# The gated experts' layer written as one flat sequence of items

## The reference

```python
x = x + _L2_ffn_ref(_layernorm(x, axis=-1), ...)

def _L2_ffn_ref(hidden, router_w, router_b, sw1, sb1, sw2, sb2, rw1, rb1, rw2, rb2):
    ...
    router_logits = flat @ router_w + router_b
    router_probs = jax.nn.softmax(router_logits, axis=-1)
    topk_probs, topk_idx = jax.lax.top_k(router_probs, TOP_K)
    weights = jnp.zeros_like(router_probs).at[jnp.arange(T)[:, None], topk_idx].add(topk_probs)
    sh = jax.nn.gelu(flat @ sw1 + sb1, approximate=False)
    shared_out = (sh @ sw2 + sb2) / N_SHARED
    h1 = jax.nn.gelu(jnp.einsum('td,edh->teh', flat, rw1) + rb1[None], approximate=False)
    expert_out = jnp.einsum('teh,ehd->ted', h1, rw2) + rb2[None]
    mixed = jnp.einsum('ted,te->td', expert_out, weights)
    return (shared_out + mixed).reshape(b, s, d)
```

## Time and profile before

| | |
|---|---|
| median of 3 runs | 1946.27 us (1944.13 to 1948.13) |
| profiled execution, its own time | 1944.69 us |
| its span, first to last instruction | 1942.6 us |
| mean granted PE clock | 0.901 of full speed |
| busy over the span | PE 1607.9 us (83%), DVE 1188.3 (61%), ACT 814.8 (42%), POOL 568.0 (29%) |
| the experts' layer in the span | from 1088.4 to about 1268 us |

### The profile page before, as it was taken

One profiled execution on the slowest core, in us unless ns is written; L12 is line 12 of the kernel. 1 busy time (PEld: TensorE's weight loads), 2 busy tenths in 40 slices (PEclk: granted clock), 3 DMA queues, 4 the chain that ended last, 5 costly groups with the idle time before them and its releaser, 6 DMA issues. The chain is left out here.

```text
span 1942.6 us, 35018 instructions
## 1 busy us (share of the span) xinstructions
PE 1607.9 (83%) x12418; PEld 1087.6 (56%) x12476; DVE 1188.3 (61%) x4278; ACT 814.8 (42%) x1765; POOL 568.0 (29%) x737
## 2 busy tenths in 40 slices
PE   6796678888789998478888799978867778999888
PEld 4474434555368777454444477745545645677556
DVE  5586454772769996445655233347848875998532
ACT  2342362664248686532545433315643400333422
POOL 2132214310144444216330000032112125777121
PEclk8887878999689998789999889979988978999999
DMA  2000004210257677306220000032110000000000
GB/s 79 12 1 10 30 1 126 57 30 1 72 192 266 230 264 242 136 14 167 60 59 11 18 1 0 1 88 58 47 64 1 1 1 1 3 3 3 1 1 22
DMA packets 81334, 115.16 MB, mean 59 GB/s; under 512 B 8464, under 2 KB 62736, under 8 KB 80400
## 3 DMA queue, kind: packets, MB, share of 16 engines
q0 software_dynamic: 18432, 67.38, 9.8%
q1 hardware_dynamic: 60144, 44.45, 8.3%
q10 hardware_dynamic: 2592, 1.18, 0.3%
HBM read 88.40 MB, written 1.05 MB: 46 GB/s over the span
## 5 line engine op out<-in xcount | busy, mean ns | idle before, releaser
L2758 POOL DMA_INDIRECT f_rows<-tree_table,f_index x128 | 129.0, 1008 | 185.5 <-PE f_ps_y L2959 89.0
L3031 ACT ACTIVATE f_rows<-f_rows,f_low_act 128x128 f32<-128x128 f32 x512 | 152.9, 386 | 0.8
L1782 ACT ACTIVATE x_probs<-x_ps_z 128x768 f32<-128x768 f32 (+1 forms) x128 | 117.3, 917 | 85.6 <-PE x_ps_z L1642 57.6
L2959 PE MATMUL f_ps_y<-f_rows,shared_sb 128*128 128x128 f32 x1024 | 128.3, 288 | 29.2 <-ACT f_rows L3031 29.2
L2959 PEld LDWEIGHTS f_ps_y<-f_rows,shared_sb 128*128 128x128 f32 x1024 | 123.7, 202 | 34.9 <-ACT f_rows L3031 31.6
L82 POOL TENSOR_TENSOR rstd<-moments,shared_sb 128x14 f32<-128x14 f32 (+3 forms) x22 | 4.6, 207 | 471.3 <-DVE moments L66 471.3
L2858 DVE CUSTOM_DVE_ANT_0 f_rows<-f_rows,f_xn 128x128 f32<-128x128 f32 x512 | 111.2, 286 | 22.8 <-DMA f_rows<-tree_table,f_index 22.8
L1472 DVE TENSOR_REDUCE x_minus_max<-x_ps_s 128x4 f32<-128x1024 f32 x64 | 77.8, 1223 | 73.0 <-PE x_ps_s L1642 72.8
L2210 PE MATMUL f_ps_h<-f_xnT,weights 128*128 128x512 f32 x144 | 77.6, 667 | 2.2 <-ACT f_hT L2275 2.2
L2275 ACT ACTIVATE f_hT<-f_ps_h,weights 128x512 f32<-128x512 f32 x72 | 48.6, 685 | 70.4 <-PE f_ps_h L2210 68.6
L2222 PEld LDWEIGHTS f_ps_y<-weights,f_hT 128*128 128x128 f32 x576 | 69.7, 192 | 14.3 <-issue 12.6
(11 more groups left out here) (666 smaller groups left out, 4106.6 us busy)
## 6 DMA issues: line engine op xcount, KB each, us to landing
x_queries<-x_pieces SPq DMA_DIRECT2D x96, 64.0 KB, 2.1
x_keys<-x_pieces SPq DMA_DIRECT2D x84, 64.0 KB, 2.1
a_queries<-a_pieces SPq DMA_DIRECT2D x48, 64.0 KB, 2.1
weights<-w_L_ffn SPq DMA_DIRECT2D x1, 2953.5 KB, 9.6
a_keys<-a_pieces SPq DMA_DIRECT2D x42, 64.0 KB, 2.1
weights<-w_L_ffn SPq DMA_DIRECT2D x1, 2449.0 KB, 9.8
weights<-w_L_ffn SPq DMA_DIRECT2D x1, 2176.0 KB, 9.0
f_rows<-tree_table,f_index POOLq DMA_INDIRECT x128, 6.0
```

The costliest lines, as they stand in the source:

```text
L1782: a.activation(probs[:, r % HELD, :, :], ps_z[:, :, 0:WIDE], ACT.Exp, scale=scale).then_inc(exped, 1)
L2758: pool.indirect_dma_start(rows[:, place(u, j), tree, :], None, g.tree_table, bass.IndirectOffsetOnAxis(index[:, u % 2, low, j * TREES + tr ...
L2959: last = pe.matmul(ps_y[:, u % SUMS, j, :], g.ident, rows[:, place(u, j), tree, OUT + f * D:OUT + (f + 1) * D], start=False, stop=(low, j, ...
L3031: last = a.activation(row, row, ACT.Copy, scale=low_act[:, u % 3, j * TREES + tree, f:f + 1])
```

## The change

The layer is written as 36 items in one sequence, with no loop: the up products of item i are followed by the down products of item i-1 across the turns' borders too. The sum banks `ps_y` become three, the `hT` buffers six, and `xnT`, `chosen`, `probs` and `chosenT` hold all tiles. The tokens of turns 2 to 4 are turned behind the ups of items 1, 2 and 3 (counted from 0). Routing is done in two batches: tiles 0 to 3 ahead of the first item, tiles 4 to 15 behind the ups of item 4, with DVE's part ahead of its addition of item 3. The router's bias becomes an addition on DVE. The chosen weights get a ninth column of ones and are turned by transposes behind items 6, 12, 13 and 14; one product per tile with a matrix of nine bias rows then opens each shared item's bank. DVE measures each turn behind its last addition and aggregates it one item into the next turn.

The diff, with removed lines shown only where they say something that the listing above does not show at a glance:

```diff
--- before.py
+++ after.py
...
-    CHUNKS = ITEMS * CH
+    ALL = TURNS * ITEMS
+    HELD, SUMS = 6, 3
+    FIRST_TILES, REST_TILES = slice(0, TILES), slice(TILES, NT)
+    TOKENS_AT = {1: 1, 2: 2, 3: 3}
+    ROUTER_AT = 4
+    CHOSEN_AT = {6: 0, 12: 1, 13: 2, 14: 3}
...
+        top, chosen = sb("top", [P, NT, 8]), sb("chosen", [P, NT, ITEMS])
+        probs, rest = sb("probs", [P, NT, E + 6]), sb("rest", [P, NT, E + 6])
+        chosenT = sb("chosenT", [ITEMS, TURNS, COLS])
+        hT = sb("hT", [P, HELD, COLS])
+        ps_t, ps_r = ps("ps_t", [P, COLS]), ps("ps_r", [P, NT, E])
+        ps_h, ps_y = ps("ps_h", [P, 2, COLS]), ps("ps_y", [P, SUMS, TILES, D])
...
+        turned = [("tokens", 0)] + [("tokens", t) for t in TOKENS_AT.values()] + [("chosen", t) for t in CHOSEN_AT.values()]
+        taken = lambda kind, t: turned.index((kind, t)) + 1
+        batch_of = lambda t: min(t, 1)
...
+            step = Chain(v, steps)
+            v.memset(chosen[:, :, E:ITEMS], 1.0)
             v.memset(probs[:, :, E:E + 6], -1.0).then_inc(padded, 1)
-            v.wait_ge(padded, 1)
...
-                v.wait_ge(routed, t + 1)
-                step(v.tensor_reduce(peak[:, :], ps_r[:, :, :], AX.X, ALU.max))
-                v.tensor_tensor(probs[:, :, 0:E], ps_r[:, :, :], per_token(peak), ALU.subtract).then_inc(shifted, 1)
...
-                for e in range(ITEMS):
-                    v.wait_ge(down_made, t * ITEMS + e + 1)
-                    if e > 0:
-                        v.wait_ge(added, t * ITEMS + e)
-                    if e < E:
...
+            def normalise_turn(t):
+                if t >= 2:
+                    v.wait_ge(xT_made, t - 1)
+                normalise(v, g, t, xn[:, t % 2, :, :]).then_inc(xn_ready, 1)
+
+            def route(batch, tiles):
+                n = tiles.stop - tiles.start
+                per_token = lambda a: a[:, tiles].rearrange("p (n o) -> p n o", o=1).broadcast_to([P, n, E])
...
+                bias = w["router_b"].rearrange("p (o e) -> p o e", o=1).broadcast_to([P, n, E])
+                v.wait_ge(routed, batch + 1)
+                step(v.tensor_tensor(odds, ps_r[:, tiles, :], bias, ALU.add))
+                step(v.tensor_reduce(peak[:, tiles], odds, AX.X, ALU.max))
+                v.tensor_tensor(odds, odds, per_token(peak), ALU.subtract).then_inc(shifted, 1)
+                v.wait_ge(exped, batch + 1)
+                step(v.tensor_reduce(total[:, tiles], odds, AX.X, ALU.add))
+                step(v.reciprocal(total[:, tiles], total[:, tiles]))
+                step(v.tensor_tensor(odds, odds, per_token(total), ALU.mult))
...
+                for j in range(tiles.start, tiles.stop):
+                    last = v.max(top[:, j, :], probs[:, j, 0:E])
+                step(last)
+                step(v.memset(top[:, tiles, 2:8], -1.0))
+                v.memset(scratch[:, :], 0.0)
+                for j in range(tiles.start, tiles.stop):
+                    last = v.match_replace(rest[:, j, :], top[:, j, :], probs[:, j, :], -2.0)
...
+                step(v.tensor_tensor(chosen[:, tiles, 0:E], rest[:, tiles, 0:E], odds, ALU.not_equal))
+                v.tensor_tensor(chosen[:, tiles, 0:E], chosen[:, tiles, 0:E], odds, ALU.mult).then_inc(chosen_ready, 1)
+
+            def add(i):
+                t, e = divmod(i, ITEMS)
+                v.wait_ge(down_made, i + 1)
+                if e == 0:
+                    v.wait_ge(chosen_ready, batch_of(t) + 1)
+                else:
+                    v.wait_ge(added, i)
+                if e < E:
+                    for j in range(TILES):
...
+                        last = v.scalar_tensor_tensor(g.x[:, n, :], ps_y[:, i % SUMS, j, :], chosen[:, n, e:e + 1],
...
+                    last = v.tensor_tensor(tiles_of(g.x, t), tiles_of(g.x, t), ps_y[:, i % SUMS, :, :], ALU.add)
+                last.then_inc(added, 1)
...
+            def measure(t):
                 v.wait_ge(added, (t + 1) * ITEMS)
-                step(take_stats(v, g, t))
-                step.end()
...
-            with v.Fori(0, TURNS - 1) as t:
-                turn(t, False)
-            turn(TURNS - 1, True)
+                take_stats(v, g, t).then_inc(stats_taken, 1)
+
+            normalise_turn(0)
+            v.wait_ge(g.loaded["L2_ffn"], 16)
+            normalise_turn(1)
+            route(0, FIRST_TILES)
+            normalise_turn(2)
+            normalise_turn(3)
+            for i in range(ALL):
+                if i == ROUTER_AT - 1:
+                    route(1, REST_TILES)
+                add(i)
+                t, e = divmod(i, ITEMS)
+                if e == E:
+                    measure(t)
+                if e == 1 and t >= 1:
+                    v.wait_ge(stats_taken, t)
+                    aggregate_behind(v, g, t, TILES)
+            v.wait_ge(stats_taken, TURNS)
+            aggregate(v, g, range((TURNS - 1) * TILES, NT)).then_inc(g.aggregated, 1)
...
-            def up(t, i):
-
-                pe.wait_ge(gelu_ready, t * CHUNKS + max(i - 1, 0))
-                pe.matmul(ps_h[:, i % 2, :], w["up"][:, i * P:(i + 1) * P], xnT[:, :], start=True, stop=True).then_inc(up_made, 1)
...
-                pe.wait_ge(gelu_ready, t * CHUNKS + CH * (e + 1))
-                pe.wait_ge(added, t * ITEMS + max(e - 1, 0))
-                if e == E:
-                    pe.wait_ge(chosenT_ready, t + 1)
...
-                    if e == E:
-                        pe.matmul(out, g.ones[0:1, 0:P], w["shared_b2"], start=False, stop=False)
-                        last = pe.matmul(out, chosenT[:, j * P:(j + 1) * P], w["expert_b2"], start=False, stop=True)
...
-                pe.wait_ge(chosenT_ready, t)
+                if t >= 1:
+                    pe.wait_ge(turned_taken, taken("tokens", t) - 1)
...
+            def turn_chosen(t):
+                pe.wait_ge(chosen_ready, batch_of(t) + 1)
+                pe.wait_ge(turned_taken, taken("chosen", t) - 1)
                 for j in range(TILES):
-                    pe.matmul(ps_r[:, j, :], xnT[:, j * P:(j + 1) * P], w["router"], start=True, stop=False)
-                    last = pe.matmul(ps_r[:, j, :], g.ones[0:1, 0:P], w["router_b"], start=False, stop=True)
+                    last = pe.transpose(ps_t[0:ITEMS, j * P:(j + 1) * P], chosen[:, t * TILES + j, :], g.ident)
+                last.then_inc(chosenT_made, 1)
+
+            def score_experts(tiles):
+                for n in range(tiles.start, tiles.stop):
+                    t, j = divmod(n, TILES)
+                    if j == 0:
+                        pe.wait_ge(turned_taken, taken("tokens", t))
+                    last = pe.matmul(ps_r[:, n, :], xnT[:, t, j * P:(j + 1) * P], w["router"], start=True, stop=True)
                 last.then_inc(routed, 1)
...
-                    if e == 5:
-                        pe.wait_ge(chosen_ready, t + 1)
-                        for j in range(TILES):
-                            last = pe.matmul(ps_t[0:E, j * P:(j + 1) * P], chosen[:, j, :], g.ident, start=True, stop=True)
-                        last.then_inc(chosenT_made, 1)
-                    if e == E and not is_last:
-                        turn_tokens(t + 1)
-                    if e > 0:
-                        down(t, e - 1)
...
+            def up(i):
+                t, e = divmod(i, ITEMS)
+                for c in range(CH):
+                    k = i * CH + c
+                    if k >= 2:
+                        pe.wait_ge(gelu_ready, k - 1)
+                    pe.matmul(ps_h[:, k % 2, :], w["up"][:, (e * CH + c) * P:(e * CH + c + 1) * P], xnT[:, t, :],
+                              start=True, stop=True).then_inc(up_made, 1)
+
+            def down(i):
+                t, e = divmod(i, ITEMS)
+                pe.wait_ge(gelu_ready, CH * (i + 1))
+                if i >= SUMS:
+                    pe.wait_ge(added, i - SUMS + 1)
+                if e == E:
+                    pe.wait_ge(turned_taken, taken("chosen", t))
+                    for j in range(TILES):
+                        pe.matmul(ps_y[:, i % SUMS, j, :], chosenT[:, t, j * P:(j + 1) * P], w["b2"], start=j == 0, stop=False)
+                for j in range(TILES):
+                    for c in range(CH):
+                        at = (e * CH + c) * P
+                        last = pe.matmul(ps_y[:, i % SUMS, j, :], hT[:, (i * CH + c) % HELD, j * P:(j + 1) * P], w["down"][:, at:at + P],
+                                         start=c == 0 and e < E, stop=c == CH - 1 and (e < E or j == TILES - 1))
+                last.then_inc(down_made, 1)
 
             turn_tokens(0)
-            with pe.Fori(0, TURNS - 1) as t:
-                turn(t, False)
-            turn(TURNS - 1, True)
+            score_experts(FIRST_TILES)
+            for i in range(ALL):
+                up(i)
+                if i in TOKENS_AT:
+                    turn_tokens(TOKENS_AT[i])
+                if i in CHOSEN_AT:
+                    turn_chosen(CHOSEN_AT[i])
```

(99 more changed lines are left out.)

57 lines of the change are left out of this document (11 added, 46 removed).

## The result

The changed kernel's median is 1917.4 us (1909.14 to 1924.45), that of the kernel before in the same comparison 1946.34 (1944.13 to 1948.13): a ratio of 0.9845, 95% interval 0.9818 to 0.9871. The profiled execution took 1909.14 us around a span of 1907.0.

The account below looks back on a forecast made before the run. PE's order of work bounds the experts' stage, with some 48 us at turn borders. Terms sum to 140.6 us against 169.6; with the head 31.2 less, minus 3.4 for a clock fall, 27.8 saved: median 1918.5 us, range 1910 to 1925.

Parts of the forecast that it names:

- Head: Before the first up product: 8 router passes of 0.262 us instead of 16, so it starts 2.1 us earlier.
- Fill: From the first up product to the third item's first: 8.45 us, kept as before.
- Items, tokens, chosen weights: On PE: 34 items at 3.50 us, token transposes 0.44 us each, four chosen-weight transposes 0.5 us a turn.
- Router's second batch: On PE, inside the item sequence: 12 tiles x 2 passes x 0.157, 3.8 us at full clock.
- Biases: Shared expert's item: four products of two passes in one run, 1.04 us a turn, 4.2 in all.
- One fall of the clock, 3.4 us: PE's clock falls once at the second router batch, costing 3.4 us and leaving 27.8 saved; chance 0.58.
- no fall: Rival: the second router batch is too short to lower the clock; 31.2 us saved, 1915.1 us; chance 0.27.
- DVE's cover and the third bank: Behind the second router batch: item 4's addition ends 0.8 us before its down needs it; two banks would be late.
- ACT's cover of 0.3 us: Behind the second router batch: item 6's Gelus, after Exp's and Gelu's table loads, end 0.3 us or more before PE needs them.
- a new wait: Rival: covers of 0.3 and 0.8 us give way, or products around transposes cost more; three us lost, about 1921.5; chance 0.10.
- Slower by the supply of instructions: Rival: straight-line code gets instructions late and each item's pitch grows; at 4.6 us about 1956 us; chance 0.03.
- Given back later: Rival: the next layer starts earlier but waits for something else, such as its weights; near 1946 us; chance 0.02.

Follow-up runs that it names:

- the repeat: The changed kernel run and profiled once more, unedited: layer 154.77 us against 153.67, median 1914.78 us, ratio 0.9855 to the kernel before.
- old_biases: Changed kernel with the shared expert's two bias products per tile put back between its down products: layer 164.78 us, median 1924.18 us, ratio 0.9901 to the kernel before.
- router_bias_pe: Changed kernel with the router's bias as a product on PE again, 48 passes in the batch: layer 166.76 us, median 1921.42 us, ratio 0.9869 to before.
- flat_alone: Changed kernel with both old kinds of bias product, in shared item and router, put back: layer 178.79 us, median 1939.26 us, ratio 0.9967 to before.
- loop_merged: Kernel before, its loops kept, with only the merged shared biases and router bias on DVE: layer 163.37 us, median 1921.95 us, ratio 0.9865 to before.

## Why the prediction was right, and which of its steps was not

The median, the direction and the range held: 1917.4 against 1918.5, inside 1910 to 1925. The steps, one by one:

- **PE's order of work bounds the layer, and the border is what goes**: held. The pitch is 3.50 as forecast and the border's step is gone.
- **Head**: forecast 2.1 less, measured 2.49. Eight router passes take 1.73, 0.216 each, not 0.262; Exp needed no table load there.
- **Fill**: forecast 8.45 kept, measured 8.30 (1091.61 to 1099.91), of which 0.44 is the token transposes I had booked apart: 0.6 less. In the repeat it is 8.66, 0.2 less.
- **Items, tokens, chosen weights**: 3.50, 0.44 and 0.44 (forecast 3.50, 0.44, 0.5).
- **Router's second batch**: forecast 3.8, measured 2.60. The term was mis-sized: 0.157 was a quarter of the 0.63 from one router product to the next in the earlier trace rows, which holds two passes over 128 rows and two of a bias product over one row. Passes of one shape have 0.108 (24 in 2.60), the same as a down pass.
- **Biases**: forecast 1.04 a turn, measured 1.09 for the run but 1.28 for the item, since the ups ahead (1.81) and the downs behind (1.88) are each 0.1 longer than elsewhere. That is 1.0 over four turns.
- **Sum from the first up product to the last addition**: forecast 140.6 without the fall, measured 139.83.
- **One fall of the clock, 3.4 us: the step that failed.** I gave it 0.58 and "no fall" 0.27. In the changed kernel the clock stays at 1.00 in and behind the router's batch. I had set a batch of 3.8 us beside 4.47 us of thin work; the batch has 2.60. The run of 48 alternating passes shows the fall, and old_biases shows it behind the same batch at half my price. So "no fall" describes the layer, and the layer saved 33.0 us where I had 27.8: 3.4 of the fall, 1.2 of the router, 0.4 of the head, 0.6 of the fill and 0.7 behind the last addition (which the repeat does not have), less 1.0 of the biases, come to 33.1.
- **The total nevertheless came out near 1918.5**: the two medians are 28.9 us apart. The rest of the program varies by some 10 us in the profiled executions, and the first four runs of the changed kernel by 15; the ratios of kernels with the same layer time give 28 to 37 us (0.9855 to 0.9811 of 1946), and 33 lies inside. The ten executions of the changed kernel in its two comparisons have a median of 1914.8, next to the 1915.1 that I gave for no fall. Whether some unprofiled executions had a fall as in old_biases can't be seen; that stays open. The accuracy of the number is partly luck; that of the terms is not.
- **DVE's cover and the third bank**: wrong in size. The chain behind Exp is 4.4 us, not 6.1: a replacement with its load takes 0.14 a tile and not 0.24, a maximum 0.08 and not 0.16. The additions of two items end at 1120.14 in one run, the first item's after half of it, at about 1118.95, and the down of the item after next starts at 1119.64. With two banks nothing waited: "this is where the third bank pays" was wrong.
- **ACT's cover of 0.3 us**: no wait, as forecast, but the cover is larger, some 1.7 us: the first Gelu of item 6 ends at 1115.73, and the ups of item 7 start at 1117.48. The batch is 1.2 shorter, and the Exp table load ran ahead of its data (1110.42, while the router was still at work).
- **The rivals**: a new wait would show as idle time of PE behind 1109; the windows have none from 1091.61 to 1130.24, and 0.03 us from there to the last addition. Slower by the supply of instructions: the pitch is 3.50 in code four times as long. Given back later: the rest of the span is not longer (1753.3 and 1758.1 against 1755.9 and 1756.7).

The Trainium skill, "TensorE: Matmul & The Clock Gate", Why this matters for your kernels, advises to keep TensorE busy without a break; read so, there would have been no fall. None came in the changed kernel; router_bias_pe, with the clock at 0.68 in 16.00 busy us out of 16.00, shows that being busy isn't enough. The Trainium skill, "TensorE: Matmul & The Clock Gate", Part 4, gives about 275 ns for a transpose in one kernel. The trace agrees as to the record of one (0.272 us in the mean for those of the chosen weights), but in a run they stand 0.11 apart, four in 0.44, and that is what the layer pays.

## What to carry to other kernels

Look for thin products first: merging two kinds of bias product and moving one to DVE brought 23.3 of 33.0 us, over twice what the flat order did, and it kept the clock up as well (1.00 in the loop's second and third turn, 0.89 to 0.93 before). A flat order pays by what stood at the border (here a table load behind an empty pipe, 1.63 us of PE's time a turn), not by the emptying itself (0.2 us). When part of a large program is edited, cut that part out of the trace and compare it, for the total scatters by 10 to 15 us here, as much as single edits bring.

## What was not expected of the hardware

- A pass's price depends on its neighbours: 0.157 us where products over 128 rows and over one row alternate, 0.108 in a run of one shape, and 0.1 us more on the ups and downs that border the bias run of nine rows.
- The same 24 router passes brought the clock down in one of five traces, and shared items with the bias products of before did so in one of four in old_biases and in three of four in flat_alone. It isn't settled what differed.
- The Exp table load started at 1110.42, 2.7 us before Exp itself could run: it did not wait for the data of the instruction that it belongs to. In loop_merged the Gelu table load at the turn's start did wait, 5.93 us, for the up product that its Gelu reads. What decides this is not shown.
